# Front shared blocks of a mixture-of-experts kernel: the down product's two weight halves joined into 512 columns, and their sums added by VectorE

## The chip, the cores and the metric

One core of a Trainium2 chip (trn2). The metric is the device time of one execution in microseconds, the median of the runs shown. Engines are named as in the profile: PE (TensorE), DVE (VectorE), ACT (ScalarE), POOL (GpSimd), SP (SyncE).

## What is computed

The reference takes 8 x 1024 rows of 256 numbers. A first layer is attention with its layernorms and a residual. The second, with which this case deals, is a feed-forward layer:

```python
scores = softmax(flat_x @ gate_w.T).T
topk_weight, topk_idx = top_k(scores, C)          # C = 1024 rows for each of 16 experts
h = gelu(xg @ Wg.T) * (xg @ Wu.T)                 # xg = flat_x[topk_idx], 1024 wide
out[topk_idx] += (h @ Wd.T) * topk_weight
shared = (gelu(x @ Sg.T) * (x @ Su.T)) @ Sd.T     # all rows, 512 wide
x = x + layernorm(out + shared)
```

## The kernel before

After the attention stage (to about 567 us) the function `moe` goes through 48 blocks of 512 rows: 12 shared blocks (numbers 0 to 11, `is_b`), 32 expert blocks (two for each of 16 experts, `is_e`) and 4 last shared blocks. All products are split in two for accuracy: each operand is a high part and a low part, and high x high, high x low and low x high are summed.

A block has steps, 4 in a shared block and 8 in an expert's (`step(b, it)`). In a step PE makes 128 hidden columns for 512 rows, twelve products of 512 columns (`up`, `mm3` at L60 to L62) into the banks psG and psU, two of each in turn. ACT takes the gelu of psG into HF (L1771), DVE multiplies psU into HF (L1983), ACT writes the high part (L1730) and DVE the low part (L1893). PE begins step s only when the product of step s - 2 is done.

After the steps comes the down product (`down(b)`), four tiles of 128 rows, with two banks of psD in turn. A shared tile is twelve products of 256 columns (`mm3` on the hidden parts and `wd_hi`, `wd_lo`); an expert's tile takes the high hidden part once with both weight halves side by side (L1634, 512 columns, eight times) and the low hidden part with the high half (L1639, 256 columns, eight times), so that the two halves of the bank hold two sums. ACT writes the tile to OUT (L1829). In a shared block this raises `s_ev`, and that is all; in an expert block it raises `s_half`, and DVE adds the second half with the row's weight (L2064) and raises `s_ev`. PE waits before tile t until `s_ev` says that tile t - 2 has left its bank.

The order is one for all engines (`schedule`): steps 2 and 3 of block b, then steps 0 and 1 of block b + 1, then `down(b)`. So down(b) of PE follows step (b+1, 1).

In the shared blocks DVE also finds the threshold of the top-k, bit by bit (`TopK`). A count (L1217) compares 1024 scores with a candidate; PE sums it over partitions (`topk.sum`, L1224); an update (L1229, L1231) makes the next candidate ahead of the next count. Thirty counts are placed by hand by the number x = s - 8: behind the step's other DVE work at x = 2, 3, 4, 5, 6 and so on, and one more at 5.5, 9.5 and so on in `down(b)`. So each of the periods of down(2) to down(7) has five. `topk.sum(s - 2)`, `(s - 1)` and `(s)` in PE's down stand ahead of tile 0, ahead of tile 2 and behind tile 3. After the counts come masks, two scans (L1278), the slots (L1291 to L1296), turned by PE (L1301), and masks of digits (L1330, L1344, L1349) that PE multiplies (L1359) and DVE accumulates (L1371 to L1376) into the index lists. In steps 0 and 1 DVE also makes the low part of the next block's rows (`x_lo`, L1880).

Blocks 0 and 1 also finish the last rows of the attention stage (`Tail`): row statistics (L971) in step (1, 1), then `v_down0` in DVE's down(0): aggregate (L976), the layernorm in two parts (L69 to L81), and a normalization (L981), which ACT shares once `s_rx` is raised (`a_down0`, L950). PE turns these rows at L894. In down(1) DVE makes a softmax (`v_shift`, `v_scores`) for which ACT gives the exponent.

SP stores each shared block's OUT when `s_ev` has all its four tiles.

Of the kernel before, what the change touches and what calls it, by code (L numbers as in the profile page):

```python
# [34 lines left out]
P = 128  # L35
# [12 lines left out]
SHIFT = 8  # L48


def wait(eng, sem, value):

    if isinstance(value, int) and value <= 0:
        return
    eng.wait_ge(sem, value)
# [41 lines left out]
class Setup:  # L97
# [116 lines left out]
    def shared_hi(self, a, i):  # L214
        w = "gud"[i]
        a.wait_ge(self.s_sh[w], 16)
        if w == "d":
            a.wait_ge(self.s_w, 4)
        a.activation(self.c.sw[w][0].rearrange("p a n -> p (a n)"), self.raw_sh[w], ACT.Copy).then_inc(self.s_whi, 1)

    def shared_lo(self, v, i):
        hi, lo = (t.rearrange("p a n -> p (a n)") for t in self.c.sw["gud"[i]])
        v.wait_ge(self.s_whi, i + 1)
        v.tensor_tensor(lo, self.raw_sh["gud"[i]], hi.bitcast(F32), ALU.subtract)

# [643 lines left out]
class Tail:  # L869
# [166 lines left out]

    def v_down0(self, v):
        self.v_aggregate(v, 1)
        v.drain()
        layernorm_scale(v, 0, self.mv[1], self.ve[:, :], self.rs[1][:, :], self.shift[1][:, :], self.tmp[:, :], NT)  # L1040
        layernorm_scale(v, 1, self.mv[1], self.ve[:, :], self.rs[1][:, :], self.shift[1][:, :], self.tmp[:, :], NT).then_inc(self.s_rx, 1)
        v.wait_ge(self.s_xnst, 16)
        v.drain()
        self.v_normalize(v, 1, self.c.XNB, self.rows, range(4, 8)).then_inc(self.s_xn[1], 1)
# [357 lines left out]
def moe(nc, io, c):  # L1402
# [7 lines left out]
    with ExitStack() as ctx:  # L1410
# [98 lines left out]
        def expert(b):  # L1509

            return (b - E0) // 2, (b - E0) % 2
# [34 lines left out]
        def _(pe):  # L1546
# [61 lines left out]
            def down(b):  # L1608
# [8 lines left out]
                if is_e(b):  # L1617
                    if expert(b)[1] == 0:
                        wait(pe, s_wlo["d"], 4 * (expert(b)[0] + 1))
                else:  # L1620
                    wd_hi, wd_lo = (bsw if is_b(b) else dsw)["d"]
                for t in range(4):
# [5 lines left out]
                    else:  # L1628
                        wait(pe, s_ev, EV0 + 4 * b + t - 1)
                    if is_e(b):  # L1630
                        for it in range(n):
                            if t == 0:
                                wait(pe, s_hhi, base[b] + it + 1)
                            pe.matmul(psD[:, t % 2, :], hidden(b, it)[0][:, t * P:(t + 1) * P],  # L1634
                                      wd_both[:, it, :, :].rearrange("p z d -> p (z d)"), start=(it == 0), stop=False)
                        for it in range(n):
                            if t == 0:
                                wait_lo(pe, b, it)
                            i = pe.matmul(psD[:, t % 2, 0:D], hidden(b, it)[1][:, t * P:(t + 1) * P], wd[0][:, it, :],  # L1639
                                          start=False, stop=(it == n - 1))  # L1640
                    else:
                        for it in range(n):
                            if t == 0:
                                wait_lo(pe, b, it)
                            h_hi, h_lo = (x[:, t * P:(t + 1) * P] for x in hidden(b, it))
                            i = mm3(pe, psD[:, t % 2, 0:D], h_hi, h_lo, wd_hi[:, it, :], wd_lo[:, it, :], it == 0, it == n - 1)
# [32 lines left out]
        def _(a):  # L1679
# [136 lines left out]
            def down(b):  # L1816
                if b < D0:
                    for t in range(4):
# [10 lines left out]
                        i = a.activation(OUT[:, t, :], psD[:, t % 2, 0:D], ACT.Copy, scale=scale)  # L1829
                        i.then_inc(s_ev if is_b(b) else s_half, 1)  # L1830
                        if b == 1 and t == 0:
# [38 lines left out]
        def _(v):  # L1870
# [102 lines left out]
            def step(b, it):  # L1973
# [12 lines left out]
                if is_b(b):  # L1986
# [3 lines left out]
                    x = s - SHIFT  # L1990
                    topk.vector_at(v, x)
                    if x in (36, 37):
# [50 lines left out]
            def down(b):  # L2043
                h = b - E0
                if b == 0:
                    tail.v_down0(v)
                if b == 1:
                    tail.v_shift(v, 1)
                    tail.v_scores(v, 1)
                if is_b(b):  # L2050
                    if b < E0 - 1:
                        topk.vector_at(v, base[b + 1] + 1.5 - SHIFT)
                    else:
                        for half in range(2):
                            sum_rows(0, half)
                if is_e(b):
                    n, tb = expert(b)
                    for t in range(4):
                        if h < NCH - AHEAD and t == 0:
                            topk.v_lo1(v, AHEAD + h)  # L2060
                        if h < NCH - AHEAD and t == 2:
                            topk.v_hival(v, AHEAD + h)
                        wait(v, s_half, 4 * h + t + 1)
                        v.scalar_tensor_tensor(OUT[:, t, :], psD[:, t % 2, D:2 * D], TW[n % 2][:, 4 * tb + t:4 * tb + t + 1], OUT[:, t, :],  # L2064
# [280 lines left out]
def build(nc, io):  # L2345
    with ExitStack() as ctx:
# [9 lines left out]
        cut = lambda t, i, k: t[:, :, :].rearrange("p a n -> p (a n)")[:, i * KD * I_SH:(i + 1) * KD * I_SH].rearrange("p (k n) -> p k n", k=k)  # L2356
        c.sw = {"g": [cut(t, 0, KD) for t in c.wg1], "u": [cut(t, 0, KD) for t in c.wu1], "d": [cut(t, 1, I_SH // P) for t in c.wg1]}
        c.XR0 = mem.over("XR0", [P, KD, 512], F32, "wu1_hi", 4 * KD * I_SH)
# [60 lines left out]
```

## Time and profile before

| | |
|---|---|
| runs | 1948.53, 1944.93, 1944.92 us; median 1944.93 |
| the profiled execution | 1946.53 us, its span 1944.7 us |
| mean granted clock of TensorE in it | 0.995 of full |
| instructions of PE, DVE, ACT | 10608 products, 2637, 1927 |

In the timeline a row is a stretch of equal instructions: start, duration, engine, line, what it writes and reads, count, and in brackets how long the engine had idled and what released it. Products on PE overlap: a product's duration is longer than the distance to the next one, and the distance is what it costs in a row. `wg_hi` and `wg_lo` are the names of the memory in which the front shared weights lie.

### The profile page before, as it was taken

Reading aid. Unit: us, or ns where it says so; the run is one execution under the profiler, and the core shown is the slowest. Engines: PE = TensorE matmul, PEld = TensorE weight load, DVE = VectorE, ACT = ScalarE, POOL = GpSimd, SP = SyncE. Lnnn points to the kernel's source line nnn. Section 1 sums busy time; section 2 is a strip of 40 time slices with the busy share of each in tenths; the row PEclk is TensorE's granted clock in tenths of the full one; section 3 lists DMA queues with packets and bytes.
Section 4 is the critical chain, followed back from the end, with each engine's and each line's share of the span. In section 5 each row is a group of like instructions: output and inputs, shape, how many; then the busy total and the mean of one; then the engine's idle time right before and its main releaser. Section 6 shows DMA issues by size and latency. Waiting matters only on the chain.

```text
span 1944.7 us, 29071 instructions
## 1 busy us (share of the span) xinstructions
PE 1919.6 (99%) x10608; PEld 1648.7 (85%) x10608; DVE 1368.2 (70%) x2637; ACT 1036.5 (53%) x1927; POOL 501.0 (26%) x595
## 2 busy tenths in 40 slices
PE   8999999999999999999999999999999999999997
PEld 6888888888888888888888888888888888888886
DVE  6777787777776888767777776757575656666657
ACT  5457576675655445445455554545454555455446
POOL 0031132033020000323432332243234323332224
PEclk9999999999999999999999999999999999999999
DMA  3113323324244111443434444443434344434566
GB/s 131 55 33 100 87 100 109 95 79 141 49 157 158 66 47 52 134 87 91 104 86 108 97 94 82 110 89 91 103 91 105 87 109 94 102 82 94 153 218 188
DMA packets 153338, 197.38 MB, mean 101 GB/s; under 512 B 104448, under 2 KB 121088, under 8 KB 145152
## 3 DMA queue, kind: packets, MB, share of 16 engines
q1 hardware_dynamic: 127824, 158.00, 26.1%
q0 software_dynamic: 25392, 37.77, 12.1%
q8 instruction: 74, 1.21, 0.3%
q14 instruction: 48, 0.39, 0.1%
HBM read 114.38 MB, written 59.34 MB: 89 GB/s over the span
## 4 chain that ended last, share of the span: by engine, by line
PE 67%; DVE 2%; DVEq 0%; issue 0%; ACT 0%; POOL 0%; POOLq 0%
PE mo_psD L1634 12%; PE mo_psG L60 8%; PE mo_psU L60 7%; PE mo_psG L61 7%; PE mo_psG L62 7%; PE mo_psU L62 7%; PE mo_psU L61 7%; PE mo_psD L1639 6%; PE mo_psD L60 1%; PE mo_psD L61 1%; PE mo_psD L62 1%; PE mo_psX L1359 1%; DVE mo_HF L1983 0%; DVE mo_F L1956 0%; PE mo_psX L900 0%
## 5 line engine op out<-in xcount | busy, mean ns | idle before, releaser
L1771 ACT ACTIVATE mo_HF<-mo_psG 128x512 f32<-128x512 f32 x320 | 191.7, 599 | 376.9 <-PE mo_psU L62 345.1
L2276 POOL DMA_INDIRECT ACC<-OUT,IDX x128 | 201.7, 1576 | 645.4 <-DVE OUT L2064 633.9
L1983 DVE TENSOR_TENSOR mo_HF<-mo_psU,mo_HF 128x512 f32<-128x512 f32 x320 | 220.2, 688 | 183.7 <-ACT mo_HF L1771 177.1
L1634 PE MATMUL mo_psD<-wd,mo_H_hi 128*128 128x512 f32 x1024 | 256.3, 392 | 0.3 <-DVE OUT L2064 0.3
L60 PE MATMUL mo_psG<-mo_XT_hi,wg_hi 128*128 128x512 f32 x640 | 253.5, 396 | 0.2 <-DVE mo_HF L1983 0.2
L60 PE MATMUL mo_psU<-mo_XT_hi,wu_hi 128*128 128x512 f32 x640 | 249.9, 390 | 0.0
L61 PE MATMUL mo_psG<-mo_XT_lo,wg_hi 128*128 128x512 f32 x640 | 249.8, 390 | 0.0
L62 PE MATMUL mo_psG<-mo_XT_hi,wg_lo 128*128 128x512 f32 x640 | 249.4, 390 | 0.0
L61 PE MATMUL mo_psU<-mo_XT_lo,wu_hi 128*128 128x512 f32 x640 | 249.1, 389 | 0.0
L62 PE MATMUL mo_psU<-mo_XT_hi,wu_lo 128*128 128x512 f32 x640 | 249.0, 389 | 0.0
L1893 DVE TENSOR_TENSOR mo_H_lo<-mo_HF,mo_H_hi 128x512 fp32r<-128x512 f32 x318 | 217.1, 683 | 0.0
L1634 PEld LDWEIGHTS mo_psD<-wd,mo_H_hi 128*128 128x128 f32 x1024 | 185.7, 188 | 35.2 <-DVE OUT L2064 0.5
L1730 ACT ACTIVATE mo_H_hi<-mo_HF 128x512 fp32r<-128x512 f32 x318 | 198.0, 623 | 6.0 <-DVE mo_HF L1983 6.0
L2064 DVE SCALAR_TENSOR_TENSOR OUT<-mo_psD,mo_TW,OUT 128x256 f32<-128x256 f32 x128 | 61.9, 483 | 185.4 <-ACT OUT L1829 185.4
L1829 ACT ACTIVATE OUT<-mo_psD,mo_TW 128x256 f32<-128x256 f32 x128 | 60.8, 475 | 239.7 <-PE mo_psD L1639 239.7
L1639 PEld LDWEIGHTS mo_psD<-wd,mo_H_lo 128*128 128x128 f32 x1024 | 141.1, 189 | 10.6
L1639 PE MATMUL mo_psD<-wd,mo_H_lo 128*128 128x256 f32 x1024 | 144.1, 284 | 0.0
L60 PEld LDWEIGHTS mo_psG<-mo_XT_hi,wg_hi 128*128 128x128 f32 x640 | 120.2, 188 | 26.6 <-DVE mo_HF L1983 3.1
L62 PEld LDWEIGHTS mo_psG<-mo_XT_hi,wg_lo 128*128 128x128 f32 x640 | 120.2, 188 | 25.7
L60 PEld LDWEIGHTS mo_psU<-mo_XT_hi,wu_hi 128*128 128x128 f32 x640 | 120.1, 188 | 25.2
L62 PEld LDWEIGHTS mo_psU<-mo_XT_hi,wu_lo 128*128 128x128 f32 x640 | 120.1, 188 | 25.1
L61 PEld LDWEIGHTS mo_psU<-mo_XT_lo,wu_hi 128*128 128x128 f32 x640 | 120.2, 188 | 24.8
(355 smaller groups left out, 3953.1 us busy)
## 6 DMA issues: line engine op xcount, KB each, us to landing
X1a<-wg_in SPq DMA_DIRECT2D x16, 1024.0 KB, 4.8
X1a<-wu_in SPq DMA_DIRECT2D x16, 1024.0 KB, 4.8
X1a<-wd_in SPq DMA_DIRECT2D x16, 1024.0 KB, 4.8
XN<-XG SPq DMA_DIRECT2D x8, 1088.0 KB, 4.1
X<-x_in SPq DMA_DIRECT2D x8, 1024.0 KB, 5.4
out_dram<-X SPq DMA_DIRECT2D x8, 1024.0 KB, 6.3
XN2T<-xn2T SPq DMA_DIRECT2D x8, 1024.0 KB, 5.1
X1a<-xt_in SPq DMA_DIRECT2D x7, 1024.0 KB, 8.6
```

The costliest lines, as they stand in the source:

```text
L60: pe.matmul(out, w_hi, x_hi, start=first, stop=False)
L61: pe.matmul(out, w_hi, x_lo, start=False, stop=False)
L62: return pe.matmul(out, w_lo, x_hi, start=False, stop=last)
L1634: pe.matmul(psD[:, t % 2, :], hidden(b, it)[0][:, t * P:(t + 1) * P], wd_both[:, it, :, :].rearrange("p z d -> p (z d)"), start=(it == 0), ...
L1639: i = pe.matmul(psD[:, t % 2, 0:D], hidden(b, it)[1][:, t * P:(t + 1) * P], wd[0][:, it, :], start=False, stop=(it == n - 1))
L1730: a.activation(hidden(b, it)[0], HF[:, it % 2, :], ACT.Copy).then_inc(s_hhi, 1)
L1771: a.activation(HF[:, it % 2, :], psG[:, it % 2, :], ACT.Gelu).then_inc(s_gelu, 1)
L1829: i = a.activation(OUT[:, t, :], psD[:, t % 2, 0:D], ACT.Copy, scale=scale)
L1893: v.tensor_tensor(lo, HF[:, it % 2, :], hi.bitcast(F32), ALU.subtract).then_inc(s_hlo, 1)
L1983: v.tensor_tensor(HF[:, it % 2, :], psU[:, it % 2, :], HF[:, it % 2, :], ALU.mult).then_inc(s_mul, 1)
L2064: v.scalar_tensor_tensor(OUT[:, t, :], psD[:, t % 2, D:2 * D], TW[n % 2][:, 4 * tb + t:4 * tb + t + 1], OUT[:, t, :], ALU.mult, ALU.add).t ...
L2276: g.indirect_dma_start(out=io["ACC"], out_offset=bass.IndirectOffsetOnAxis(ap=c.IDX[:, n, 4 * tb + t:4 * tb + t + 1], axis=0), in_=OUT[:, ...
```

## The change

The shared down weights are laid side by side (`sd_both`), the front shared blocks use the expert's form of the down product, ACT's eviction raises `s_half` for them too, and DVE adds the second half of the bank (`add_halves`) and raises `s_ev`. `v_down0` is cut in two. In steps with it = 1 (but not of block 0) the call of `topk.vector_at` moves into `down(b)`, behind two adds. The last four shared blocks keep the old form.

```diff
-    def v_down0(self, v):
-        self.v_aggregate(v, 1)
-        v.drain()
-        layernorm_scale(v, 0, ...)
+    def v_down0(self, v, part):
+        if part == 0:
+            self.v_aggregate(v, 1)
+            v.drain()
+            layernorm_scale(v, 0, ...)
+            return
         layernorm_scale(v, 1, ...).then_inc(self.s_rx, 1)
...
# PE, down(b)
-                    if is_e(b):
+                    if b < D0:
                         for it in range(n):
...
                             pe.matmul(psD[:, t % 2, :], hidden(b, it)[0][:, t * P:(t + 1) * P],
-                                      wd_both[:, it, :, :].rearrange("p z d -> p (z d)"), start=(it == 0), stop=False)
+                                      both[:, it, :, :].rearrange("p z d -> p (z d)"), start=(it == 0), stop=False)
...
-                            i = pe.matmul(psD[:, t % 2, 0:D], hidden(b, it)[1][:, t * P:(t + 1) * P], wd[0][:, it, :],
+                            i = pe.matmul(psD[:, t % 2, 0:D], hidden(b, it)[1][:, t * P:(t + 1) * P], both[:, it, 0, :],
...
# ACT, down(b)
-                        i.then_inc(s_ev if is_b(b) else s_half, 1)
+                        i.then_inc(s_half, 1)
...
# DVE, step(b, it)
-                    topk.vector_at(v, x)
+                    if it != 1 or b == 0:
+                        topk.vector_at(v, x)
...
# DVE, down(b)
+                def add_halves(ts):
+                    for t in ts:
+                        wait(v, s_half, 4 * b + t + 1)
+                        v.tensor_tensor(OUT[:, t, :], psD[:, t % 2, D:2 * D], OUT[:, t, :], ALU.add).then_inc(s_ev, 1)
+
                 if b == 0:
-                    tail.v_down0(v)
-                if b == 1:
+                    add_halves(range(1))
+                    tail.v_down0(v, 0)
+                    add_halves(range(1, 2))
+                    tail.v_down0(v, 1)
+                    topk.vector_at(v, base[b + 1] + 1 - SHIFT)
+                    add_halves(range(2, 4))
+                elif b == 1:
                     tail.v_shift(v, 1)
+                    add_halves(range(1))
                     tail.v_scores(v, 1)
+                    add_halves(range(1, 2))
+                    topk.vector_at(v, base[b + 1] + 1 - SHIFT)
+                    add_halves(range(2, 4))
+                elif is_b(b):
+                    add_halves(range(2))
+                    if b < E0 - 1:
+                        topk.vector_at(v, base[b + 1] + 1 - SHIFT)
+                        if base[b + 1] + 1 - SHIFT < 26:
+                            add_halves(range(2, 4))
+                    else:
+                        add_halves(range(2, 4))
                 if is_b(b):
                     if b < E0 - 1:
                         topk.vector_at(v, base[b + 1] + 1.5 - SHIFT)
+                        if base[b + 1] + 1 - SHIFT >= 26:
+                            add_halves(range(2, 4))
...
-                        wait(v, s_half, 4 * h + t + 1)
+                        wait(v, s_half, 4 * b + t + 1)
...
# build
-        c.sw = {"g": [cut(t, 0, KD) for t in c.wg1], "u": [cut(t, 0, KD) for t in c.wu1], "d": [cut(t, 1, I_SH // P) for t in c.wg1]}
+        c.sd_both = mem.over("sd", [P, I_SH // P, 2, D], F32R, "wg1_hi", 4 * KD * I_SH)
+        c.sw = {"g": [cut(t, z, KD) for z, t in enumerate(c.wg1)], "u": [cut(t, 0, KD) for t in c.wu1], "d": [c.sd_both[:, :, z, :] for z in (0, 1)]}
```

## Rows read from the trace of the kernel before

**Rows 1.** The page: busy us, share of the span, instructions.

```profile
PE 1919.6 (99%) x10608; PEld 1648.7 (85%) x10608; DVE 1368.2 (70%) x2637; ACT 1036.5 (53%) x1927; POOL 501.0 (26%) x595
```

**Rows 2.** PE's waits over the span: us in total, times, longest us.

```profile
PE mo_psG L894 <- PEq L229: 2.2, 1, 2.2
PE psS L374 <- ACT X1a L471: 1.1, 2, 0.9
```

**Rows 3.** Timeline of ACT, down(3) and the step behind it; gelus and evictions.

```profile
652.93 0.60 ACT L1771 ACTIVATE mo_HF<-mo_psG 128x512 f32<-128x512 f32 x1 [1.08 <-PE mo_psU L62]
...
658.86 0.39 ACT L1829 ACTIVATE OUT<-mo_psD 128x256 f32<-128x256 f32 x1 [1.03 <-PE mo_psD L62]
...
670.13 0.60 ACT L1771 ACTIVATE mo_HF<-mo_psG 128x512 f32<-128x512 f32 x1 [1.08 <-PE mo_psU L62]
```

**Rows 4.** Timeline of DVE around down(3).

```profile
654.71 0.68 DVE L1983 TENSOR_TENSOR mo_HF<-mo_psU,mo_HF 128x512 f32<-128x512 f32 x1
...
656.52 0.15 DVE L1229 SCALAR_TENSOR_TENSOR mo_off<-mo_psX,mo_BT 128x1 int32<-128x1 f32 x1
...
662.35 0.69 DVE L1983 TENSOR_TENSOR mo_HF<-mo_psU,mo_HF 128x512 f32<-128x512 f32 x1 [1.62 <-ACT mo_HF L1771]
...
672.14 0.69 DVE L1983 TENSOR_TENSOR mo_HF<-mo_psU,mo_HF 128x512 f32<-128x512 f32 x1
```

**Rows 5.** Timeline of PE, down(0): the first products of tiles 0 and 2.

```profile
591.95 0.28 PE L60 MATMUL mo_psD<-wg_hi,mo_H_hi 128*128 128x256 f32 x1
...
594.81 0.28 PE L60 MATMUL mo_psD<-wg_hi,mo_H_hi 128*128 128x256 f32 x1
```

**Rows 6.** Timeline of PE, the first expert block's down product.

```profile
823.66 1.98 PE L1634 MATMUL mo_psD<-wd,mo_H_hi 128*128 128x512 f32 x8
825.48 1.13 PE L1639 MATMUL mo_psD<-wd,mo_H_lo 128*128 128x256 f32 x8
826.44 2.01 PE L1634 MATMUL mo_psD<-wd,mo_H_hi 128*128 128x512 f32 x8
...
829.25 2.01 PE L1634 MATMUL mo_psD<-wd,mo_H_hi 128*128 128x512 f32 x8
```

**Rows 7.** Instructions on psD: ns min/median/max, first and last start us.

```profile
L1947 DVE TENSOR_TENSOR mo_F<-mo_psD,mo_F x16: 410/418/425, 1883.7 to 1933.3; 128x256 f32<-128x256 f32 x16
```

**Rows 8.** Timeline of DVE around down(0).

```profile
597.56 0.65 DVE L976 BATCH_NORM_AGGREGATE mo_tail_mv<-mo_tail_st 128x2 f32<-128x6 f32 x8
...
599.50 0.17 DVE L74 TENSOR_TENSOR mo_tail_tmp<-mo_tail_rs 128x8 f32<-128x8 f32 x1
...
603.75 0.69 DVE L1983 TENSOR_TENSOR mo_HF<-mo_psU,mo_HF 128x512 f32<-128x512 f32 x1 [1.15 <-ACT mo_HF L1771]
```

**Rows 9.** Timeline of PE behind step (1, 3).

```profile
603.29 1.09 PE L894 MATMUL mo_psX<-ident,XG 128*128 128x128 f32 x8
604.59 0.47 PE L60 MATMUL mo_psG<-mo_XT_hi,wg_hi 128*128 128x512 f32 x1 [0.20 <-DVE mo_HF L1983]
```

**Rows 10.** Timeline of PE, down(3): the sums ahead of tile 2 and behind tile 3.

```profile
655.70 0.17 PE L1224 MATMUL mo_psX<-mo_cnt,mo_same_r 128*128 128x2 f32 x1
...
658.66 0.17 PE L1224 MATMUL mo_psX<-mo_cnt,mo_same_r 128*128 128x2 f32 x1
```

**Rows 11.** Timeline of PE and DVE, down(8): PE's tile 2, DVE's slots.

```profile
742.66 0.37 PE L60 MATMUL mo_psD<-wg_hi,mo_H_hi 128*128 128x256 f32 x1
...
743.61 0.15 DVE L1291 TENSOR_SCALAR mo_OFF<-mo_psX 128x2 f32<-128x2 f32 x1
```

**Rows 12.** Timeline of DVE and ACT, down(9).

```profile
761.86 0.68 DVE L1880 TENSOR_TENSOR mo_XT_lo<-mo_XR,mo_XT_hi 128x512 fp32r<-128x512 f32 x1
...
761.92 0.39 ACT L1829 ACTIVATE OUT<-mo_psD 128x256 f32<-128x256 f32 x1 [1.04 <-PE mo_psD L62]
```

**Rows 13.** Timeline of PE behind down(10): the first turn of an expert's rows.

```profile
786.17 1.03 PE L1557 MATMUL mo_psX<-ident,mo_XG 128*128 128x128 f32 x8
```

**Rows 14.** Stretch, its us, busy us of PE, PEld, DVE, ACT, POOL, granted clock, DMA share, GB/s.

```profile
566.90:570.30 3.40, 3.40 (x19) 3.40 (x18) 0.29 (x1) 2.23 (x5) 0.64 (x2) 0.56 0.72 231
```

More of the change, by code:

```diff
@@ L218, in shared_hi @@
             a.wait_ge(self.s_w, 4)
-        a.activation(self.c.sw[w][0].rearrange("p a n -> p (a n)"), self.raw_sh[w], ACT.Copy).then_inc(self.s_whi, 1)
+        hi = self.c.sw[w][0]
+        a.activation(hi, self.raw_sh[w].rearrange("p (a n) -> p a n", a=hi.shape[1]), ACT.Copy).then_inc(self.s_whi, 1)
     def shared_lo(self, v, i):
-        hi, lo = (t.rearrange("p a n -> p (a n)") for t in self.c.sw["gud"[i]])
+        hi, lo = self.c.sw["gud"[i]]
         v.wait_ge(self.s_whi, i + 1)
-        v.tensor_tensor(lo, self.raw_sh["gud"[i]], hi.bitcast(F32), ALU.subtract)
+        v.tensor_tensor(lo, self.raw_sh["gud"[i]].rearrange("p (a n) -> p a n", a=hi.shape[1]), hi.bitcast(F32), ALU.subtract)
 def attention(nc, io, c):
@@ L1035, in v_end @@
             self.v_stats(v, 1, x, range(4))
-    def v_down0(self, v):
-        self.v_aggregate(v, 1)
-        v.drain()
-        layernorm_scale(v, 0, self.mv[1], self.ve[:, :], self.rs[1][:, :], self.shift[1][:, :], self.tmp[:, :], NT)
+    def v_down0(self, v, part):
+        if part == 0:
+            self.v_aggregate(v, 1)
+            v.drain()
+            layernorm_scale(v, 0, self.mv[1], self.ve[:, :], self.rs[1][:, :], self.shift[1][:, :], self.tmp[:, :], NT)
+            return
         layernorm_scale(v, 1, self.mv[1], self.ve[:, :], self.rs[1][:, :], self.shift[1][:, :], self.tmp[:, :], NT).then_inc(self.s_rx, 1)
@@ L1619, in down @@
                         wait(pe, s_wlo["d"], 4 * (expert(b)[0] + 1))
+                    both = wd_both
                 else:
-                    wd_hi, wd_lo = (bsw if is_b(b) else dsw)["d"]
+                    both, (wd_hi, wd_lo) = c.sd_both, dsw["d"]
                 for t in range(4):
@@ L2356, in build @@
         cut = lambda t, i, k: t[:, :, :].rearrange("p a n -> p (a n)")[:, i * KD * I_SH:(i + 1) * KD * I_SH].rearrange("p (k n) -> p k n", k=k)
-        c.sw = {"g": [cut(t, 0, KD) for t in c.wg1], "u": [cut(t, 0, KD) for t in c.wu1], "d": [cut(t, 1, I_SH // P) for t in c.wg1]}
+        assert mem.place["wg1_lo"] == mem.place["wg1_hi"] + 2 * 4 * KD * I_SH
+        c.sd_both = mem.over("sd", [P, I_SH // P, 2, D], F32R, "wg1_hi", 4 * KD * I_SH)
+        c.sw = {"g": [cut(t, z, KD) for z, t in enumerate(c.wg1)], "u": [cut(t, 0, KD) for t in c.wu1], "d": [c.sd_both[:, :, z, :] for z in (0, 1)]}
         c.XR0 = mem.over("XR0", [P, KD, 512], F32, "wu1_hi", 4 * KD * I_SH)
```

## The prediction

> **What bounds the kernel now.** I read the busy shares first, then PE's waits, then the timeline of the stretch that the change touches. PE is busy for 99% of the span [rows 1]. Behind the start of the kernel it waited 2.2 us once, ahead of the front shared blocks, and 0.9 us at most in the attention stage [rows 2]; the list of its waits has none of over 0.3 us in the shared blocks themselves. There a block takes 17.2 us, from the gelu at 652.93 to the one at 670.13 [rows 3], and PE issues through all of it. So what is saved on PE is gained, and what PE must wait for is lost.
>
> DVE has little room there. In the six blocks with counts (downs of blocks 2 to 7) its one long idle time in a period is 1.62 us, before the product of step (b+1, 2) [rows 4]. It lies behind the down product, not beside its first tiles: at 652.93, when PE starts on the down product, DVE is still at the count of the step before; the HF product of step (b+1, 1) starts at 654.71, though its gelu began at 652.93, and the split of the next block's rows keeps DVE until 656.52 [rows 3, 4]. A change that puts DVE between a tile of the down product and the reuse of its bank meets this backlog.
>
> **PE's own work.** The change turns, per tile, twelve products of 256 columns into four of 512 and four of 256. Today two tiles take 594.81 - 591.95 = 2.86 us, so one takes 1.43 [rows 5]. The expert's tile is the new mix twice over: eight and eight, 829.25 - 826.44 = 2.81 us, half of it 1.405 [rows 6]. That saves 0.023 us a tile, 1.1 us in 48 tiles. The bounds: with the 0.2275 us of the first expert tile's 512-column products, (825.48 - 823.66)/8, a tile takes 4 x 0.2275 + 4 x 0.12 = 1.39 and 1.9 us are saved; below, nothing is saved. I take 1.1, since the row with the same mix is nearest. The columns are the same, 3072 a tile; only the cost per instruction falls.
>
> The rows show about 12 ns over the bare column time for each product (1.43/12 = 0.119 against 256 columns at 2.4 GHz, 0.107). The Trainium skill, TensorE: Matmul & The Clock Gate, section Back-to-back issue gap, gives an isolated product a floor of about 2.5 ns beside its columns; by that the join would save an estimated 0.5 us in all, which speaks against the change even on its own ground. The rows disagree with it in size, and the sum goes by the rows.
>
> **The evictions.** Today ACT reads a tile's 256 sums and frees its bank. Now ACT copies one half, DVE adds the other, and only the add raises s_ev; PE needs add t-2 before tile t. The nearest add of this shape, at the end of the kernel, takes 0.418 us [rows 7]; after it I allow 0.1 us until PE issues (the nearest restart: DVE's 0.69 us product from 603.75 ends at 604.44 and PE's first product stands at 604.59, 0.15 [rows 8, 9]; nothing would be the other end). An undisturbed tile needs 0.20 us from PE's end to ACT (658.66 to 658.86), 0.39 for ACT, 0.06, 0.42 and 0.1, together 1.17, under the 1.40 of the tile between: no wait where DVE stands ready. It mostly doesn't.
>
> *Count blocks, six of them.* PE's tile 1 ends at 655.70, where the sum stands [rows 10]. Tile 2 could start at 655.70 - 0.05 + 0.12 (the sum) = 655.77. The diff moves the count of step (b+1, 1) behind two adds, but the count of step (b+1, 0), which makes the backlog, stays. So add 0 starts at 656.52, ends at 656.94, and PE goes on at 657.04: 1.27 us lost. Add 1 ends by 657.30, before tile 3 asks. The moved count runs from 657.2 to 659.0, in time for the sum behind tile 3 at 659.85. Adds 2 and 3 wait for ACT: the last ends at 660.9, and the count of the half step at 662.7, just when PE's sum at the start of step (b+1, 3) asks for it (659.97 and a step of 2.73 later). The product of step (b+1, 2) would start at 663.5; DVE idles 0.8 us again, so nothing piles up. But over the next steps DVE falls behind as before (its product of the next step with it = 1 stands at 672.14, 2.0 us after the gelu at 670.13 began), and the next down product meets the same backlog. The loss comes back each time: 6 x 1.27 = 7.6 us.
>
> *Block 0.* DVE takes row statistics until 597.56, then starts the aggregate [rows 8]. Tile 2 could start at 594.76 and waits for add 0 until 598.08: 3.3 us. The first part of the layernorm, 599.50 - 597.56 = 1.94 us, stands between the adds, so add 1 ends near 600.3 and tile 3, ready at 599.5, waits 0.9 more. Of these 4.2 us, 0.6 come back: the down product ends at 594.81 + 2.86 = 597.67 and two steps of 12 x 0.2275 us at 603.13, so PE stood 0.2 us before the turn at 603.29 and, with eight transposes of some 0.11, 0.4 before the product at 604.59, behind ACT and DVE [rows 9]. Net 3.6.
>
> *Block 1.* DVE has no count there and waits for ACT's exponent anyway; its adds go around that wait: nothing.
>
> *Block 8.* The second scan leaves DVE at the split until 743.61; add 0 ends at 744.03, PE goes on at 744.13 rather than at 742.66 [rows 11]: 1.5 us. The slot work moves by two adds (0.7) and still ends before PE asks for it a step later.
>
> *Block 9.* DVE is in the digit masks; the split starts at 761.86 and ends its issue 0.60 later, at 762.46 [rows 12]. ACT's third eviction is at 761.92, so tile 2 started near 760.3. Add 0 frees the bank at 762.98: 2.7 us.
>
> *Block 10.* DVE works without a pause from the down product to the accumulation that PE's turn of the first expert's rows waits for, up to PE's transposes at 786.17 [rows 13]. All four adds stand ahead of it: 4 x 0.35 (back to back) = 1.4 us. Block 11: DVE is free, nothing.
>
> Moved DMAs: SP's stores of a block's sums wait for the last add, 1 to 7 us later than now. Behind them on SP's queue stand the loads of rows, which serve a block two further on (over 17 us), and the first index lists, which are made later than the store before them. I cost this at nothing; with that cover gone PE's turn of the first gathered rows would come later by as much as the store did, in block 10 by the two counts of masks between its adds, some 4 us.
>
> Stalls 7.6 + 3.6 + 1.5 + 2.7 + 1.4 = 16.8, less 1.1 saved: 15.7 us.
>
> **The clock.** When PE had stood 2.2 us before its first transposes at L894 [rows 2], the granted clock fell to its lower level, 1.2 of 2.4 GHz, and was 0.56 of full on the mean of the 3.4 us from 566.90 [rows 14]; PE's 0.9 us waits in the attention stage left it full. The stalls in block 9 (2.7) and block 0 (3.3) are longer than 2.2. 0.44 of 3.4 us is 1.5 lost in block 9; in block 0 PE waits again meanwhile, so some 0.8. Together 2.3. The 1.27 us stalls lie nearer to the 0.9 row, and I give them nothing.
>
> Sum: 15.7 + 2.3 = 18.0 us. The profiled execution took 1946.53, 1.6 above the median of 1944.93; by the median the forecast is 1962.9 us.
>
> **The rivals.**
> *The adds fit.* DVE's idle 1.62 us a period is more than four adds at 0.35. If the adds found DVE free, only the 1.1 us on PE would show: 1943.8. This decides at one point, whether the split of step (b+1, 1) is issued before PE ends tile 1: by 655.8 rather than 656.52. Against it stands that the HF product starts 1.8 us late in every period. For more than 0.2% (3.9 us, about what a measurement of this kernel can tell from no change) the join would have to save 20 ns a product pair; the upper bound above is 10. So this is mostly "same".
> *Stalls without a fall of the clock.* 15.7 us, 1960.6. For it: one row of a fall is little, and it stands where one stage ends and the next begins.
> *The clock falls at every stall.* Six times 1.5 more, 9 us: 1972. For it: a stall of 1.27 us lies between 0.9 (no fall) and 2.2 (fall).
>
> **How the numbers follow.** Forecast 0.50, stalls alone 0.25, clock at every stall 0.15, adds fit 0.10. Slower by over 0.2% takes the first three, 0.90; within 0.2% gets 0.07, faster by over it 0.03. The range: below, the stalls alone with restarts at once and the larger saving (ten stalls x 0.1 and 0.8 less) and smaller slips, 1957; above, the clock at every stall and a little over it, 1973. It leaves out the last rival and little else.
>
> **What would show it.** PE's waits should list the first 512-column down product waiting for the new add about ten times: six of 1.1 to 1.4 us, one over 3 us near 595, one of 2.7 near 760. The period of the count blocks should be 18.3 to 18.4 instead of 17.2; a tile without a wait 1.40; and the expert stage should be as long as before. I am wrong if DVE's idle time before the adds ends on ACT's copy rather than PE's on the add, if the period stays at 17.2 or less, or if the clock rows show more than two new falls.

## The result, and the profile after

The changed kernel takes 1964.25 us (median of 4, 1962.45 to 1965.17), the kernel before 1944.93 (median of 4): 19.3 us longer, a ratio of 1.0096 with a 95% interval of 1.0084 to 1.0108. The profiled execution took 1963.77 us, 17.2 more than that of before (1946.53).

The page's busy times, against [rows 1]: PE is busy 2.7 us longer with 192 products fewer (4 for each of 48 tiles), DVE 17.5 us longer with 48 instructions more (the adds).

```profile
PE 1922.3 (98%) x10416; PEld 1640.0 (84%) x10416; DVE 1385.7 (71%) x2685; ACT 1036.2 (53%) x1927; POOL 501.4 (26%) x595
```

PE's waits, against [rows 2]: us in total, times, longest us. L1638 is the 512-column down product, L2054 the new add.

```profile
PE mo_psD L1638 <- DVE OUT L2054: 14.9, 10, 3.0
PE mo_psG L895 <- PEq L230: 2.2, 1, 2.2
PE psS L375 <- ACT X1a L472: 0.9, 1, 0.9
PE mo_psX L1560 <- DVE mo_vf L1379: 0.3, 1, 0.3
PE mo_psX L1227 <- DVE mo_junk L1220: 0.2, 1, 0.2
```

Ten waits on the new add, 14.9 us. The timeline of PE shows where (down 0, 4, 8, 9, 10; the other five count blocks have the row of down 4), against [rows 5, 11]:

```profile
592.01 1.08 PE L1638 MATMUL mo_psD<-sd,mo_H_hi 128*128 128x512 f32 x4
...
593.40 1.09 PE L1638 MATMUL mo_psD<-sd,mo_H_hi 128*128 128x512 f32 x4
...
597.92 2.08 PE L1638 MATMUL mo_psD<-sd,mo_H_hi 128*128 128x512 f32 x4 [2.95 <-DVE OUT L2054]
...
600.65 1.29 PE L1638 MATMUL mo_psD<-sd,mo_H_hi 128*128 128x512 f32 x4
...
681.11 1.19 PE L1638 MATMUL mo_psD<-sd,mo_H_hi 128*128 128x512 f32 x4 [1.16 <-DVE OUT L2054]
...
756.17 1.21 PE L1638 MATMUL mo_psD<-sd,mo_H_hi 128*128 128x512 f32 x4 [1.29 <-DVE OUT L2054]
...
776.43 1.21 PE L1638 MATMUL mo_psD<-sd,mo_H_hi 128*128 128x512 f32 x4 [2.54 <-DVE OUT L2054]
...
796.69 1.20 PE L1638 MATMUL mo_psD<-sd,mo_H_hi 128*128 128x512 f32 x4 [1.11 <-DVE OUT L2054]
```

Each time it is tile 2, which needs the bank of tile 0. The timeline of DVE in down(4), against [rows 4], shows the backlog: DVE is at the count until 678.9, then takes product, low part and split, and adds only at 680.64. ACT had copied tile 0 at 678.59.

```profile
677.63 1.28 DVE L1220 TENSOR_SCALAR_CACHE_REDUCE mo_junk<-mo_SCT,mo_cand 128x1024 bf16<-128x1024 f32 x1
678.84 0.08 DVE L1220 DVE_READ_ACCUMULATOR mo_junk<-mo_SCT,mo_cand 128x1 fp32r x1
678.84 0.69 DVE L1987 TENSOR_TENSOR mo_HF<-mo_psU,mo_HF 128x512 f32<-128x512 f32 x1
679.44 0.68 DVE L1897 TENSOR_TENSOR mo_H_lo<-mo_HF,mo_H_hi 128x512 fp32r<-128x512 f32 x1
680.04 0.69 DVE L1884 TENSOR_TENSOR mo_XT_lo<-XR,mo_XT_hi 128x512 fp32r<-128x512 f32 x1
680.64 0.75 DVE L2054 TENSOR_TENSOR OUT<-mo_psD,OUT 128x256 f32<-128x256 f32 x2
...
684.62 0.42 DVE L2054 TENSOR_TENSOR OUT<-mo_psD,OUT 128x256 f32<-128x256 f32 x1 [0.97 <-ACT OUT L1833]
...
687.66 0.69 DVE L1987 TENSOR_TENSOR mo_HF<-mo_psU,mo_HF 128x512 f32<-128x512 f32 x1 [0.89 <-ACT mo_HF L1775]
```

DVE's one idle time of 1.62 us has become two here, of 0.97 and 0.89 us. DVE still has room; it has it in the wrong place.

A table of the first eviction of each down product in the timeline of ACT says what each block costs. The distance from one down to the next, after less before, in us:

| from down | 0 | 1 | 2 | 3 | 4 | 5 | 6 | 7 | 8 | 9 | 10 |
|---|---|---|---|---|---|---|---|---|---|---|---|
| before | 24.25 | 19.12 | 17.20 | 17.20 | 17.27 | 17.20 | 17.20 | 17.39 | 18.64 | 18.63 | 18.84 |
| longer | 3.92 | -0.10 | 1.34 | 1.69 | 1.24 | 1.39 | 1.33 | 1.21 | 1.42 | 2.73 | 1.23 |

Together 17.4 us: 3.9 in block 0, 8.2 in the six count blocks, 5.4 in blocks 8 to 10. Of the profiled difference of 17.2 nothing is left for the expert blocks. The granted clock, in three stretches (columns as in [rows 14]): block 0's tile 2, down(1) with its softmax, and block 9's tile 2.

```profile
597.80:601.20 3.40, 3.28 (x10) 2.80 (x11) 2.57 (x19) 0.31 (x1) 0.00 (x0) 0.52 0.04 17
618.00:625.00 7.00, 7.00 (x26) 6.13 (x26) 2.98 (x9) 2.27 (x4) 0.00 (x0) 0.51 0.05 19
776.40:779.80 3.40, 3.37 (x36) 2.86 (x38) 0.31 (x1) 0.60 (x2) 0.00 (x0) 1.00 0.00 0
```

So the clock fell to its lower level (1.2 of 2.4 GHz) once more than before, in block 0. Behind the 2.54 us of block 9 it did not fall. The stretch in down(1) stands in the profiled execution of before too; it comes up again below.

### The profile page after: what moved, and what is told of

It is laid out like the page before. It is cut to its first block, busy times and chain, and to the rows that moved or that the text cites. A ratio compares the mean times of both kernels' runs of the same rounds, so it can differ in the third digit from the quotient of the medians.

```text
span 1962.0 us, 28735 instructions
## 1 busy us (share of the span) xinstructions
PE 1922.3 (98%) x10416; PEld 1640.0 (84%) x10416; DVE 1385.7 (71%) x2685; ACT 1036.2 (53%) x1927; POOL 501.4 (26%) x595
## 4 chain that ended last, share of the span: by engine, by line
PE 64%; DVE 5%; issue 1%; DVEq 1%; ACT 0%; POOL 0%; POOLq 0%
PE mo_psD L1638 13%; PE mo_psG L60 7%; PE mo_psU L60 7%; PE mo_psG L61 7%; PE mo_psG L62 7%; PE mo_psU L62 7%; PE mo_psU L61 7%; PE mo_psD L1643 7%; DVE mo_HF L1987 1%; DVE mo_H_lo L1897 1%; DVE mo_junk L1220 0%; DVE mo_XT_lo L1884 0%; PE mo_psX L1362 0%; DVE mo_F L1960 0%; DVE mo_hi L1347 0%
## 5 line engine op out<-in xcount | busy, mean ns | idle before, releaser
L1638 PE MATMUL mo_psD<-wd,mo_H_hi 128*128 128x512 f32 x1024 | 256.3, 392 | 0.3 <-DVE OUT L2094 0.3
L1638 PEld LDWEIGHTS mo_psD<-wd,mo_H_hi 128*128 128x128 f32 x1024 | 185.7, 188 | 35.2 <-DVE OUT L2094 0.5
```

## The experiments

My theory: the whole loss is PE's wait for a bank that DVE frees late, because DVE has a backlog where tile 0's add is due; the join itself gives about 1 us. Against it: the moved count or the join cost something by themselves, the loss is a fixed number of DVE instructions whatever their place, or it sits in one block.

In the diffs JOIN is the set of blocks that have the joined product and the adds; a block outside it is as before, its count in its old place too (only the weights lie side by side everywhere). FIRST is the set of those in which the adds go ahead of DVE's other work. Twelve runs fell on three chips: the first four on one where the kernel before takes 1945.12 us, the next four on one where it takes 1951.34, the last four on a third with 1951.38. On which chip the two profiles above were taken is not known; the kernel before took 1944.93 us there and has none of the ACT waits told below, as on the first chip, so they are called the first chip's. Each ratio is against the kernel before on its own chip, and is worked out from the single runs, not from the two medians.

**The adds left out.** ACT frees the bank, as before; the second half of the bank is not read.

```diff
-                        i.then_inc(s_half, 1)
+                        i.then_inc(s_half if is_e(b) else s_ev, 1)
...
-                    for t in ts:
+                    for t in ():
```

> The joined products stay; VectorE's 48 adds are left out (so the product of the high hidden part with the low weight half is missing from the output), and ACT's eviction frees the bank again, as before the change. The count of the step with it = 1 stays in the down product. My theory (PE waits for adds that stand behind VectorE's backlog): all ten waits of PE go, the count blocks' period is 17.1 us, tiles without a wait 1.40 us, and the time is about 1 us under the kernel before, 1944. Rival (the moved count or the joined products themselves cost the time): it stays near 1960 or, for the moved count alone, 2 to 7 us above the kernel before.

Measured: 1944.58 us against 1945.12, ratio 0.9998 (0.9988 to 1.0007). All ten waits are gone. The moved counts, the joined products and the cut `v_down0` together cost nothing that can be measured. They give little either: the six distances from down(2) to down(8) are 103.23 us together, against 103.46 before. In down(0), where no sum stands between the tiles, a tile takes 1.40 as forecast (593.26 - 591.86). In down(4) two tiles and a sum take 2.93 us, against 2.96 before [rows 10], where twice 0.023 would have given 2.91. And the sum behind tile 3 has a row of 0.27 instead of 0.16 there: DVE's count ends at 673.96, just when PE asks for it. That is so in this one block of six, and the kernel before has a like row (0.24) at the same sum:

```profile
668.12 0.17 PE L1227 MATMUL mo_psX<-mo_cnt,mo_same_r 128*128 128x2 f32 x1
...
671.05 0.16 PE L1227 MATMUL mo_psX<-mo_cnt,mo_same_r 128*128 128x2 f32 x1
...
674.02 0.27 PE L1227 MATMUL mo_psX<-mo_cnt,mo_same_r 128*128 128x2 f32 x1
```

**The count blocks alone.**

```diff
+        JOIN, FIRST = set(range(2, 8)), set(())
```

> The joined form with its adds only in the six count blocks (downs of blocks 2 to 7), the old form in the other six. My theory: six waits of 1.16 us, 7.0, less 24 tiles at 0.023, 0.6: some 6.4 us over the kernel before, 1951.3, and no fall of the clock in block 0. Rival (the stalls in the other blocks depend on those here, or these do on the delay that block 0 brings): the waits are shorter or longer than 1.16 us.

Measured: 1952.28 us, +7.2, ratio 1.0046 (1.0029 to 1.0063); one of the four runs, at 1957.01, lifts the ratio. The granted clock stays full in block 0. PE waits six times on the add, five times 1.16 us and once 1.21:

```profile
PE mo_psD L1640 <- DVE OUT L2059: 7.0, 6, 1.2
```

The price of the count blocks stands by itself: 1.2 us each by the medians, 1.3 by the six distances (111.48 us together, against 103.46).

**The add ahead of the backlog.** All blocks joined; in blocks 2 to 7 the same instructions in another order. Add 0 goes ahead of the product of step (b+1, 1), add 1 behind its low part, then the count, then the split of the rows.

```diff
+        JOIN, FIRST = set(range(12)), set(range(2, 8))
...
# DVE, step(b, it)
+                if it == 1 and b - 1 in FIRST:
+                    add_halves_of(b - 1, range(1))
...
+                if it == 1 and b - 1 in FIRST:
+                    add_halves_of(b - 1, range(1, 2))
...
-                    if it != 1 or b == 0:
+                    if it != 1 or b == 0 or b - 1 not in JOIN or b - 1 in FIRST:
                         topk.vector_at(v, x)
+                    if it == 1 and b - 1 in FIRST and b < E0 - 1:
+                        x_lo(b + 1, it)
```

> The kernel after, with the same instructions in another order in the six count blocks: VectorE's add 0 stands ahead of the HF product of step (b+1, 1), add 1 behind the low hidden part, the moved count behind that and the split of the next rows last. My theory (only add 0's place behind 1.9 us of other VectorE work makes PE wait): the six waits of 1.16 us go, the time falls by 7 us to 1957, and four waits (3.0, 1.4, 2.5, 1.0) are left. Rival (the chain PE, ACT, VectorE, PE is itself longer than a tile, or VectorE is full in these blocks): waits move to tile 3 or to the sums behind it, and the time falls by less than 3 us.

Measured: 1957.66 us, +12.5, ratio 1.0068 (1.0051 to 1.0085). That is 7 us less than the changed kernel's 19.3, with not one DVE instruction fewer (2685 in both). Of the ten waits four are left, those of blocks 0, 8, 9 and 10:

```profile
PE mo_psD L1640 <- DVE OUT L2059: 7.9, 4, 3.0
```

So most of the loss of the count blocks is place, not work. What stays is some 0.25 us a period (17.42 to 17.46 in five of them and 17.78 in one, against 17.20): in each period two sums have the 0.27 us row, where the changed kernel has one, because DVE's count ends only as PE asks for it (at 680.58 and 683.58). PE's timeline, the sum behind tile 3 and the one a step later:

```profile
680.63 0.27 PE L1227 MATMUL mo_psX<-mo_cnt,mo_same_r 128*128 128x2 f32 x1
...
683.64 0.27 PE L1227 MATMUL mo_psX<-mo_cnt,mo_same_r 128*128 128x2 f32 x1
```

**The old products with the adds.** Twelve 256-column products a tile, as before; ACT's copy raises `s_half`, and the add reads the first half of the bank.

```diff
-                    if b < D0:
+                    if is_e(b):
...
-                        v.tensor_tensor(OUT[:, t, :], psD[:, t % 2, D:2 * D], OUT[:, t, :], ALU.add)
+                        v.tensor_tensor(OUT[:, t, :], psD[:, t % 2, 0:D], OUT[:, t, :], ALU.add)
```

> The kernel after with the twelve products of 256 columns of the kernel before in the front shared blocks; the adds stay where they are but read the first half of the bank (so that the first sum is added twice). My theory (the join saves 0.023 us a tile and no more): 1.1 us over the kernel after, less what the waits hide, so 0.5 to 1.1: 1965. Rival (the join saves by the number of instructions, some 0.1 us for each of four a tile): near 1980.

Measured: 1964.69 us, ratio 1.0107 (1.009 to 1.0124), as long as with the join: the intervals overlap. PE's waits:

```profile
PE mo_psD L60 <- DVE OUT L2059: 15.3, 11, 2.9
```

An eleventh wait of 0.8 us came up in block 1. The adds make the loss; the shape of the products hardly matters.

**Block 0 alone.**

```diff
+        JOIN, FIRST = set((0,)), set(())
```

> The change in block 0 alone (v_down0 still cut in two, adds at their places); blocks 1 to 11 as before. My theory: the two waits of PE stand there alone, 2.95 us before tile 2 and about 0.9 before tile 3, and the granted clock falls for some 3.4 us near 598, as in the changed kernel and in neither the kernel with counts only nor the one without adds. Price of the stalls 3.9 less about 0.6 given back, and some 0.8 for the clock: about +4 us, 1949.0. Rival (the clock fall belongs to something else than this wait, or costs nothing because PE waits again meanwhile): +3.2, 1948.1. Rival (the next steps absorb the wait, since DVE and ACT catch up): under +2.

Measured: 1956.13 us against 1951.34, +4.8, ratio 1.0024 (1.0015 to 1.0033). PE's timeline and two stretches with the granted clock:

```profile
597.91 2.07 PE L1640 MATMUL mo_psD<-sd,mo_H_hi 128*128 128x512 f32 x4 [2.96 <-DVE OUT L2059]
...
600.63 1.21 PE L1640 MATMUL mo_psD<-sd,mo_H_hi 128*128 128x512 f32 x4
```

```profile
597.30:600.70 3.40, 2.79 (x9) 2.41 (x10) 2.71 (x18) 0.00 (x0) 0.00 (x0) 0.53 0.19 80
618.00:625.00 7.00, 7.00 (x35) 7.00 (x35) 2.45 (x8) 2.24 (x4) 0.00 (x0) 0.51 0.05 19
```

The clock's fall in block 0 belongs to this wait. The 0.9 us wait before tile 3 is not there: tile 2 ran at the lower clock, took 2.7 us instead of 1.4, and add 1 was done meanwhile. Part of the stall was paid by the clock.

**Block 0 with its two adds together.**

```diff
-                    add_halves(range(1))
+                    add_halves(range(2))
                     tail.v_down0(v, 0)
-                    add_halves(range(1, 2))
                     tail.v_down0(v, 1)
```

> As the kernel with block 0 alone, but adds 0 and 1 stand together ahead of v_down0, so that tile 3 does not wait for the first part of the layernorm. My theory: PE waits once, about 2.95 us, and not before tile 3; if the clock's fall comes from the one long wait, it falls here too. About 0.7 us under the kernel with the adds apart: 1948.3. Rival (the fall needs both waits, one shortly behind the other): no fall here, and about 1.5 us under it, 1947.5. Rival (add 1 ahead of v_down0 waits for ACT's eviction of tile 1, so the aggregate is late and PE's transposes of the tail's rows wait longer): no gain.

Measured: 1955.67 us, +4.3, ratio 1.0019 (1.0009 to 1.0028), not to be told from the run above. The clock falls here too, so one wait is enough for it:

```profile
597.40:600.80 3.40, 2.93 (x9) 2.56 (x10) 2.71 (x19) 0.00 (x0) 0.00 (x0) 0.51 0.16 65
```

I had expected a gain of 0.7 from a wait saved before tile 3. There was no such wait to save, as the run above shows.

**Blocks 8 to 10 alone.**

```diff
+        JOIN, FIRST = set((8, 9, 10)), set(())
```

> The change in blocks 8, 9 and 10 alone (scan, slots and digit masks); blocks 0 to 7 and 11 as before. My theory, from the trace of the changed kernel: waits of PE on the add of 1.3 us in block 8, 2.5 in block 9 and, in block 10, no wait of PE on an add but the accumulation late by the four adds, some 1.2; no new fall of the clock: +5.4, 1950.4. Rival (the 2.5 us wait lowers the clock as the 2.95 one did, when it stands alone): 1.5 more, 1951.9. Rival (in block 9 and 10 the digit masks are bound by DVE as a whole, so that the waits are one and the same delay and not three): +4 or less, 1949.

Measured: 1961.34 us, +10.0, ratio 1.0052 (1.0036 to 1.0067), nearly twice what was expected. The three waits on the add are those of the changed kernel (4.9 us, longest 2.5), the one in block 10 too, which I had expected at the accumulation and not at an add. Two things came on top. In block 8 the clock fell behind the 1.29 us wait, at 0.54 over 3.4 us, where it had stayed full in the changed kernel. And in block 10 PE waited 2.9 us for DVE's accumulation, behind which the clock fell too, for some 3.4 us from 793:

```profile
742.40:745.80 3.40, 3.17 (x10) 2.75 (x11) 3.23 (x6) 0.20 (x1) 0.00 (x0) 0.54 0.00 0
```

```profile
PE mo_psX L1562 <- DVE mo_vf L1379: 2.9, 1, 2.9
```

DVE itself stood idle for 2.6 us ahead of that accumulation, and the view names nothing of this core's engines that it waited for ("remote").

**ACT frees the bank.** Blocks 0 to 8 joined. ACT copies all 512 sums of a tile to scratch memory and raises `s_ev`; DVE adds all four tiles in one operation at the end of `down(b)`, and the counts stand where they stood before.

```diff
# ACT
+                            a.activation(SCR[:, t, :], psD[:, t % 2, :], ACT.Copy).then_inc(s_ev, 1)
...
# DVE, down(b), behind the half step's count
+                            wait(v, s_ev, EV0 + 4 * (b + 1))
+                            wait(v, s_st, 16 * b)
+                            v.tensor_tensor(OUT[:, :, :], SCR[:, :, 0:D], SCR[:, :, D:2 * D], ALU.add).then_inc(s_fin, 1)
...
# SP
+                    wait(sp, s_fin, done(b) + 1)
```

> The joined products in blocks 0 to 8, but ACT copies all 512 sums of a tile (both halves) to scratch memory and frees the bank itself; DVE adds the halves of all four tiles in one operation of 1024 elements a partition, at the end of down(b), behind the half step's count, and the counts stand where they stood before. Blocks 9 to 11 keep 256-column products. My theory (the whole loss is the bank's wait for DVE, and DVE has room of 1.6 us a period behind the down product): no wait of PE on an add, a period of 17.1 in the count blocks, and the joined tiles' 0.023 us each show: 36 tiles, 0.8 us, so 1944.1. Rival (DVE's add of about 1.1 us at the end of down(b) delays the product of step (b+1, 2) by more than its idle time, and PE waits for it each period): +0.3 to 0.5 a block, 1947 to 1949. Rival (ACT's copy of 512 sums takes 0.6 instead of 0.4 us and the bank comes back later than the 1.40 us of a tile): not expected, 0.2 + 0.6 + 0.1 is under 1.40.

Measured: 1950.56 us against 1951.34, 0.8 less, ratio 0.9996 (0.9987 to 1.0005). No wait of PE on an add. The timeline of PE gives the join's worth at the sums:

```profile
668.63 0.17 PE L1227 MATMUL mo_psX<-mo_cnt,mo_same_r 128*128 128x2 f32 x1
...
671.56 0.16 PE L1227 MATMUL mo_psX<-mo_cnt,mo_same_r 128*128 128x2 f32 x1
...
674.50 0.16 PE L1227 MATMUL mo_psX<-mo_cnt,mo_same_r 128*128 128x2 f32 x1
```

Two tiles and a sum take 2.93 and 2.94 us, against 658.66 - 655.70 = 2.96 before [rows 10]. ACT's copy and DVE's late add fit in:

```profile
670.36 0.59 ACT L1841 ACTIVATE mo_SCR<-mo_psD 128x512 f32<-128x512 f32 x1
```

```profile
676.48 1.22 DVE L2074 TENSOR_TENSOR OUT<-mo_SCR 128x1024 f32<-128x1024 f32 x1
678.19 0.69 DVE L1999 TENSOR_TENSOR mo_HF<-mo_psU,mo_HF 128x512 f32<-128x512 f32 x1 [0.49 <-ACT mo_HF L1780]
```

The six distances of the count blocks are 103.20 us together, against 103.46 before: of all orders tried that form and add both sums there, this is the only one in which these blocks are not longer than before. Its gain is below what can be measured.

What was open now: blocks 8 to 10 had cost nearly twice the expected sum, on another chip. The next three runs went to that. They were meant for that same chip and fell on a third, which is like it.

**The kernel before, profiled on the third chip.** No edit.

> The kernel before, unchanged, for a profile on the same chip as the runs beside it. The chip that ran block 0 alone and blocks 8 to 10 alone had the kernel before at 1951.3 instead of 1945.1, and traces with some 40 idle times of ACT of 2.3 us that end on nothing in the profile. Theory (that chip's instruction streams are slower, whatever the kernel): if the job falls on it, about 1951 with the same idle times of ACT in the expert blocks and none of PE in the shared blocks; on a chip like the first, 1945 without them. Rival (they come from the edits): 1945 and none, on any chip.

Measured: 1951.01 us, one run. ACT's waits over the span have a kind that the profile from the first chip does not have; "issue" means that the profile shows nothing that the engine waited for:

```profile
ACT OUT L1829 <- issue: 90.9, 39, 2.3
```

PE has six waits of 0.5 to 0.6 us for DVE's product, 68.5 us apart, in the expert blocks, and one of 0.4 at 789, which the first chip's profile does not have; block 10 is 1.0 us longer there (19.81 from down to down, against 18.84). The 6 us by which this chip is slower are at least in part there, and they are no part of the change.

**The changed kernel on the third chip.** No edit.

> The changed kernel, unchanged, on the same chip as the kernel with blocks 8 to 10 alone. My theory (parts add up: counts 7.3, block 0 4.7, blocks 8 to 10 5.4): 17 to 19 us over the kernel before on either chip, ten waits of the same lengths, and in block 10 no idle time of DVE that ends on nothing. Rival (the chip, not the kernel with blocks 8 to 10 alone, made that kernel's cost 10): a like idle time of some 2.6 us in block 10 here too, and 4 us more: 22.

Measured: 1973.07 us, +21.7, ratio 1.0105 (1.0089 to 1.0122). The ten waits are as long as in the first profile, but for the one in block 0 (3.2, 1.16 six times, 1.29, 2.54, 1.11), and the idle time of DVE in block 10 is there. The clock fell in block 0 and, behind the wait that this idle time makes, in block 10:

```profile
804.50 0.26 DVE L1377 TENSOR_TENSOR mo_vf<-mo_psX,mo_vf 64x64 f32<-64x64 f32 x1 [2.34 <-remote]
```

```profile
805.25 1.94 PE L1560 MATMUL mo_psX<-ident,mo_XG 128*128 128x128 f32 x8 [2.69 <-DVE mo_vf L1379]
```

```profile
804.40:811.20 6.80, 5.95 (x18) 5.07 (x19) 3.94 (x11) 2.20 (x4) 0.00 (x0) 0.51 0.12 31
```

Block 10 is 6.1 us longer than in the profile of before from this chip. The adds' 1.2, this wait of 2.7 and half of the 6.8 us at the lower clock would make 7.3; the kernel before loses 1.0 of that here too. On the first chip it was 1.2.

**Blocks 8 to 10 once more.** No edit to the first such run.

> The change in blocks 8, 9 and 10 alone, once more. Of its first cost of 10 us, 5.3 were expected; the trace showed beside the three waits on the add an idle time of DVE of 2.6 us in block 10 that ends on nothing in the profile (PE waited 2.9 for the accumulation behind it, and the granted clock fell), and a fall of the clock in block 8. Theory (the idle time belongs to that chip, the waits to the change): on a chip on which the kernel before takes 1945, +5.4 and at most one fall more, 1950 to 1952, and no wait of PE of over 1 us on the accumulation. Rival (both belong to this order of instructions): +10 on any chip.

Measured: 1960.46 us, +9.1, ratio 1.0047 (1.003 to 1.0064). From down to down blocks 8, 9 and 10 are 1.39, 2.68 and 4.77 us longer than in the profile of before on the same chip. The clock stayed full in block 8 this time; the 1.29 us wait before it was the same:

```profile
742.40:745.80 3.40, 3.36 (x18) 2.93 (x19) 3.23 (x5) 0.64 (x2) 0.00 (x0) 1.00 0.00 0
```

The idle time in block 10 is there a third time (2.35 us, ahead of the same instruction). So the surplus of some 3.5 to 4.5 us is the change on this kind of chip, not one kernel's accident. The run fell on the slower kind of chip, so by itself it does not part the chip from the order of instructions, as it was meant to; that is done by the first chip's three profiles with adds in block 10, which have no such idle time.

**The best order with DVE's adds.** Joined in blocks 1 to 8 and 11; in 2 to 8 add 0 goes ahead of the backlog.

```diff
+        JOIN, FIRST = set([1, 2, 3, 4, 5, 6, 7, 8, 11]), set(range(2, 9))
```

> The joined products in blocks 1 to 8 and 11 alone, and in blocks 2 to 8 add 0 stands ahead of the HF product of step (b+1, 1) and add 1 behind the low part, ahead of the count and the split. Blocks 0, 9 and 10 keep 256-column products and their eviction by ACT. My theory (what is left is the 0.25 us a period that the sums wait for the counts): 7 x 0.25 + some 0.2 less 36 x 0.023, +1.1 over the kernel before; no wait of PE on an add over 0.3. Rival (the early adds delay the low part of the hidden values for the next tile, and the loss comes back elsewhere): +3 or more. Rival (it is faster, as the joined product is meant to be): -1.

Measured: 1952.50 us, +1.1, ratio 1.0004 (0.9995 to 1.0014), as expected, though the interval does not part it from no change. No wait of PE on an add over 0.3 us. In its profile the six count blocks are 1.5 us longer than in that of before, as expected (0.25 each), and block 10, which is not joined, 0.5.

## Why the prediction was right

The forecast was 1962.9 us, +18.0; the median is 1964.25, +19.3, inside the range, on the side that had 0.90. Point by point, by the distances between evictions:

- *DVE's backlog delays tile 0's add, and PE loses it* (the step on which the sign hung): right. The split was issued at 680.04, the add at 680.64 and PE's tile 2 at 681.11. The six waits of the count blocks and those of blocks 8 and 9 came as forecast, and moving the adds ahead took the six away. That there are ten in all is partly luck: the second wait of block 0 did not come, and one in block 10 did that I had put elsewhere.
- *Count blocks, 6 x 1.27 = 7.6 us, less the join*: the forecast of the stall holds, the sum is 8.2. In down(4) the sum ahead of tile 2 stands at 679.79 in PE's timeline and the product at 681.11, where it would follow by 0.03 without a wait: 1.29 lost. (The idle time in the rows, 1.16, starts from a modelled end.) Six times that is 7.7. The term that was missed is one costed at nothing: adds 2 and 3 and the half step's count were to come "just when PE's sum at the start of step (b+1, 3) asks for it". They come later. That sum has a row of 0.24 to 0.27 us in each of the six blocks, and in down(3) it waited 0.2 besides; with it down(3) is the table's 1.69. This eats the join's gain and more:

```profile
668.32 0.27 PE L1227 MATMUL mo_psX<-mo_cnt,mo_same_r 128*128 128x2 f32 x1 [0.20 <-DVE mo_junk L1220]
```

- *The join, 0.023 us a tile*: where sums stand between the tiles, the two-tile stretch shortened by 0.02 to 0.03 us instead of 0.046, so 0.010 to 0.015 a tile; for all 48 tiles that would be 0.5 to 0.7 us. Down(0) has no sums, like the expert's tile, and there the forecast 1.40 holds (593.40 - 592.01 = 1.39 in the changed kernel). Why a sum takes part of the gain is not shown.
- *Block 0, 3.6 + 0.8 for the clock*: measured 3.9. The wait before tile 2 was 2.95 (3.3 forecast), the one before tile 3 did not come, and the clock fell as forecast. The two effects overlap where I had added them. The 3.9 is too small, though: the profile of before has a long low stretch of the clock in down(1), see the last point. From down 0 to down 2 the seven other profiles without the late add and without that stretch take 41.7 to 41.9 us, the profile of before 43.4, and the changed kernel 47.2. Against the seven block 0 costs 5.4, where 4.4 was forecast.
- *Block 9, 2.7 + 1.5 for the clock*: the stall is right (2.73), the fall of the clock did not come. This step failed. That a wait of over 2.2 us lowers the clock was read from one row.
- *Blocks 8 and 10, 1.5 and 1.4*: measured 1.42 and 1.23 on the first chip. In block 10 the size is right and the place is not: PE lost it at tile 2, in a wait of 1.11 for the new add, and not at the turn of the expert's rows, where it waited 0.3. *Block 1 and SP's later stores at nothing*: right, -0.10, and no wait of PE in the shared or expert blocks beyond 0.3 but the ten on the new add.
- *The profiled execution of before lies 1.6 above its median, so the difference is taken by profile*: this is where 19.3 and 17.2 part; 0.5 more comes from the changed kernel's profiled execution, which lies below its median. In the profile of before the clock is low for 6.8 us in down(1), in the one from the third chip for 3.4, if the low level is half of the full one ((0.46 + 0.39) x 4 / 0.5 and (0.39 + 0.03) x 4 / 0.5), as two stretches of 4 us show, first of the former, then of the latter:

```profile
614.00:618.00 4.00, 4.00 (x22) 4.00 (x22) 1.95 (x5) 0.00 (x0) 0.00 (x0) 0.54 0.11 41
618.00:622.00 4.00, 4.00 (x24) 4.00 (x24) 1.01 (x4) 2.36 (x4) 0.00 (x0) 0.61 0.00 0
```

```profile
614.00:618.00 4.00, 4.00 (x24) 4.00 (x24) 1.87 (x5) 0.32 (x1) 0.00 (x0) 0.61 0.11 43
618.00:622.00 4.00, 4.00 (x35) 4.00 (x34) 1.01 (x4) 2.31 (x5) 0.00 (x0) 0.97 0.04 15
```

Half of the 3.4 us between them is 1.7, about the 1.6 above the median. Six profiled kernels had a late add in block 0, the changed one on two chips among them, and five had the long stretch; of the eight others one had it. So the wait in block 0 seems to make the long stretch in down(1) frequent, and this is a cost of the change that the profiled pair hides. It is counted over fourteen single profiles, not tested.

How near the sum came is partly luck. By the profiled pair the count blocks cost 8.2 where 7.6 less the join's 0.5 was forecast, and block 9 cost 2.7 where 4.1 was; these two misses, of 1.1 and 1.4, take each other off. And the long stretch in the profile of before hid some 1.6 of block 0's cost, which came back in the medians.

One reading behind the sum was loose too. The product of step (b+1, 1) was called 1.8 us late by counting from the start of its gelu; where DVE is free it starts 0.63 behind that (662.35 against 661.72 in the trace of before), so the lateness is 1.2. No term used it.

The rivals: "the adds fit" is refuted by the ten waits. "The clock falls at every stall" is refuted by the clock rows, though the stall of 1.29 us in block 8 did lower it in one profile of six. "Stalls without a fall of the clock" gave 1960.6; it missed the fall in block 0. The forecast had two falls and one came, so on the clock the truth lies between the two.

## What to carry to other kernels

When the engine that frees a PSUM bank changes, ask what that engine is doing at the moment when the bank is due, not how busy it is: DVE had 1.6 us idle in each period, and PE still lost 1.2, because the idle time came some 5 us after the add was wanted. Price the place of an instruction ahead of its duration: here the adds of six blocks, moved ahead of a product, its low part and a split of rows, took 7 us off. And when the gain is 10 to 23 ns a tile, free the bank on the engine that freed it before, or leave the products alone.

## What the runs showed of the hardware

- The granted clock does not follow the length of a wait alone. It fell behind the wait of 2.9 to 3.2 us in block 0 (six profiles of six) and that of 2.7 to 2.9 in block 10 (three of three), behind the 1.29 us of block 8 in one of six, and never behind the 2.5 us of block 9, in six. Behind the 2.2 us ahead of the front shared blocks it fell in thirteen profiles of fourteen; the changed kernel on the third chip has the same 2.18 us wait there and a clock of 1.00 over 566 to 574. The Trainium skill, TensorE: Matmul & The Clock Gate, section What's actually happening, says that the activity is judged on a clock of its own, not from the kernel's start; the same 1.29 us wait with and without a fall, at 742 us in two runs of one kernel, agrees.
- A fall of the clock can hide a second stall: tile 2 of block 0 took 2.7 us instead of 1.4, and the wait before tile 3 vanished.
- Chips differ in more than speed. On two of three chips ACT shows some 40 idle times of 2.3 us that end on nothing which the profile shows, the kernel before takes 6 us more, and DVE has one such idle time of 2.3 to 2.6 us at the same instruction of block 10 in all three profiles with adds there. It delays PE; in the kernel before on the third chip one of 1.1 us falls a few instructions later, and PE waits 0.4 us. What it is stays open: no run here tells the loading of instructions from another cause.
